# Combine weights of a top-2 expert layer: stored to DRAM from the token-major table, without a transposition on TensorE

## What is computed

```python
mod = (_silu(L0_c) @ L0_wmod).reshape(L0_c.shape[0], 6, 1, -1)
...
h = _layernorm(x, axis=-1) * (1 + ca) + sa
x = x + ga * _L0_attn_ref(h, L0_attn_w_qkv, L0_attn_w_out)     # 16 heads of 8 channels
h = _layernorm(x, axis=-1) * (1 + cb) + sb
x = x + gb * _L0_ffn_ref(h, L0_ffn_w_router, L0_ffn_w_gate, L0_ffn_w_up, L0_ffn_w_down)
...
scores = jax.nn.softmax(xf @ w_router, axis=-1)                # 8 experts
topk_w, topk_idx = jax.lax.top_k(scores, TOP_K)                # 2
topk_w = topk_w / (jnp.sum(topk_w, axis=-1, keepdims=True) + EPS)
comb = jnp.zeros((T, E), dtype=xf.dtype).at[jnp.arange(T)[:, None], topk_idx].set(topk_w)
h = jax.nn.silu(g) * u                                         # per expert, 176 hidden
out_e = jnp.einsum('eth,ehd->etd', h, w_down)
y = jnp.einsum('etd,te->td', out_e, comb)
```

## Time and profile before

| what | value |
|---|---|
| median of 3 runs | 687.15 us (686.04 to 687.64) |
| span of the profiled execution | 679.4 us |
| its own time | not listed apart; the median is 7.75 us above the span |
| TensorE busy | 618.9 us (91%) |
| VectorE busy | 550.1 us (81%) |
| ScalarE busy | 450.5 us (66%) |
| GpSimd busy | 267.2 us (39%) |
| transfers | 65.58 MB in 48972 packets, 97 GB/s |

### The profile page before, as it was taken

One profiled execution on the slowest core, in us unless ns is written; L12 is line 12 of the kernel. 1 busy time (PEld: TensorE's weight loads), 2 busy tenths in 40 slices (PEclk: granted clock), 3 DMA queues, 4 the chain that ended last, 5 costly groups with the idle time before them and its releaser, 6 DMA issues.

```text
span 679.4 us, 13009 instructions
## 1 busy us (share of the span) xinstructions
PE 618.9 (91%) x3413; PEld 285.7 (42%) x3413; DVE 550.1 (81%) x1065; ACT 450.5 (66%) x859; POOL 267.2 (39%) x384
## 2 busy tenths in 40 slices
PE   5299999999999999999999999889899999999995
PEld 3112223323323322322322322225667777777773
DVE  3698889899888988988988988714788888888885
ACT  2107878778778778778778777876554555555553
POOL 4522022222222222222122122333567776776773
PEclk9658999999999999999999999979899999999999
DMA  7703505304304304303403400253334454345411
GB/s 183 197 31 82 183 3 117 106 20 106 117 19 95 126 17 95 127 17 79 143 18 72 150 18 4 76 167 109 92 114 139 137 142 141 130 137 150 136 35 31
DMA packets 48972, 65.58 MB, mean 97 GB/s; under 512 B 9432, under 2 KB 30432, under 8 KB 48928
## 3 DMA queue, kind: packets, MB, share of 16 engines
q1 hardware_dynamic: 46304, 64.32, 33.1%
q10 hardware_dynamic: 2624, 0.79, 0.5%
HBM read 47.26 MB, written 17.83 MB: 96 GB/s over the span
## 4 chain that ended last, share of the span: by engine, by line
PE 34%; DVE 20%; issue 19%; POOL 16%; ACT 5%; DMA 2%; SPq 1%; DVEq 1%; POOLq 0%; ACTq 0%
POOL hid_lo L612 13%; DVE negmax L864 13%; PE o_acc L1172 11%; PE s_row L1149 10%; PE s_col L1162 5%; ACT probs L656 3%; DVE probs L1042 1%; POOL h_lo L618 1%; PE misc L1130 1%; PE misc L1103 1%; PE misc L1100 1%; SPq L325 1%; DVE sums_inv L883 1%; DVE k_rest L878 1%; PE misc L1126 1%
## 5 line engine op out<-in xcount | busy, mean ns | idle before, releaser
L864 DVE TENSOR_REDUCE negmax<-s_row 128x1 f32<-128x512 f32 x512 | 323.0, 683 | 47.5 <-PE s_row L1149 41.9
L656 ACT ACTIVATE probs<-s_col 128x512 f32<-128x512 f32 x512 | 270.8, 599 | 76.4 <-PE s_col L1162 73.4
L1149 PE MATMUL s_row<-k_stack,q_stack 64*128 64x512 bf16 x512 | 141.7, 402 | 25.2 <-DMA k_stack<-k_scr 11.6
L612 POOL TENSOR_TENSOR hid_lo<-probs,hid_hi 128x512 fp32r<-128x512 f32 x87 | 128.5, 1493 | 61.9 <-ACT hid_hi L800 61.9
L1162 PE MATMUL s_col<-q_stack,k_stack 64*128 64x512 bf16 x512 | 132.4, 383 | 7.1 <-ACT probs L656 6.5
L1172 PE MATMUL o_acc<-probs,v_aug 128*32 128x512 f32 x1024 | 138.1, 612 | 0.0
L800 ACT ACTIVATE hid_hi<-probs 128x512 fp32r<-128x512 f32 x88 | 55.6, 632 | 85.0 <-DVE probs L1042 84.6
L1149 PEld LDWEIGHTS s_row<-k_stack,q_stack 64*128 64x128 bf16 x512 | 34.9, 93 | 180.1 <-DVE negmax L864 142.1
L1042 DVE TENSOR_TENSOR probs<-probs,q_stack 128x512 f32<-128x512 f32 x56 | 62.5, 1116 | 15.7 <-POOL hid_lo L612 13.6
L520 POOL CAST negmax_parts<-negmax 128x16 bf16<-128x16 f32 x32 | 6.3, 196 | 163.0 <-DVE negmax L864 163.0
L1032 DVE TENSOR_TENSOR probs<-probs,s_col 128x512 f32<-128x512 f32 x88 | 59.6, 677 | 2.9 <-ACT probs L820 1.6
(11 more groups left out here) (134 smaller groups left out, 713.9 us busy)
## 6 DMA issues: line engine op xcount, KB each, us to landing
q_scr<-q_parts SPq DMA_DIRECT2D x48, 128.0 KB, 2.4
k_scr<-k_parts SPq DMA_DIRECT2D x48, 128.0 KB, 2.4
q_stack<-q_scr SPq DMA_DIRECT2D x8, 768.0 KB, 6.1
k_stack<-k_scr SPq DMA_DIRECT2D x8, 768.0 KB, 7.5
q_stack<-combT_scr SPq DMA_DIRECT2D x24, 256.0 KB, 3.4
k_stack<-combT_scr SPq DMA_DIRECT2D x16, 224.0 KB, 2.9
q_stack<-combT_scr SPq DMA_DIRECT2D x16, 192.0 KB, 2.7
q_stack<-combT_scr SPq DMA_DIRECT2D x16, 160.0 KB, 2.6
```

What stands on the lines that cost most here:

```text
L612: nc.gpsimd.tensor_tensor(hid_lo[k % HIDDEN][:], weighed[(par + k) % 2], hid_hi[k % HIDDEN][:], ALU.subtract).then_inc(s["hid_split"], 1)
L656: nc.scalar.activation(probs[t % 2][:, j, :], s_col[score_bank("col", u)][:], ACT.Exp, scale=INV_SCALE).then_inc(s["exp_done"], 1)
L864: nc.vector.tensor_reduce(negmax[n % 2][:, j, qc:qc + 1], s_row[score_bank("row", u)][:], AX.X, ALU.max, negate=True).then_inc(s["row_max" ...
L1149: nc.tensor.matmul(s_row[score_bank("row", u)][:], q_stack[par][at:at + KS, head // 2, P * qc:P * (qc + 1)], k_stack[par][at:at + KS, head ...
```

## The change

The store of the combine weights reads `comb` itself: for each of the 4 chunks one transfer whose source is [128 tokens, 8 experts] and whose destination is `combT_scr` by expert, so consecutive elements of four bytes lie 2 KB apart in DRAM. The task `combT` is taken out of both tables, with TensorE's transposes, ScalarE's copy, the tile `combT` and the semaphore `combT_ready`. SyncE waits for `comb_step` instead, GpSimd's `combine` waits for the stores of the batch before, and every wait on `combT_kept` counts four transfers a batch.

```diff
@@ TASKS, OUTPUT, TAIL_AT
-        (12, 1): "max0", (15, 0): "combT",
+        (12, 1): "max0",
-    OUTPUT = ("o0", "o1", "o2", "o3", "attnT", "proj", "x1T", "router", "combT")
+    OUTPUT = ("o0", "o1", "o2", "o3", "attnT", "proj", "x1T", "router")
-               (6, 1): "x1T", (7, 1): "router", (10, 1): "combT"}
+               (6, 1): "x1T", (7, 1): "router"}
-        combT = sb("combT", [E, N])
@@ SyncE
             def keep_combT(b):
-                sp.wait_ge(s["combT_ready"], b + 2)
+                sp.wait_ge(s["comb_step"], 2 * (b + 1))
                 sp.sem_inc(s["waited"])
-                sp.dma_start(combT_scr[bass.ds(b, 1)].rearrange("o e n -> e (o n)"), combT[:]).then_inc(s["combT_kept"], 16)
+                with nc.allow_non_contiguous_dma(reason="4096 weights, by expert in DRAM"):
+                    for k in range(CH):
+                        sp.dma_start(combT_scr[bass.ds(b, 1), :, P * k:P * (k + 1)].rearrange("o e p -> p (o e)"), comb[:, k, :]).then_inc(s["combT_kept"], 16)
...
-                        sp.wait_ge(s["combT_kept"], 16)
+                        sp.wait_ge(s["combT_kept"], 16 * CH)
...
-                        sp.wait_ge(s["combT_kept"], 16 * (b + 1))
+                        sp.wait_ge(s["combT_kept"], 16 * CH * (b + 1))
@@ GpSimd
-                pool.wait_ge(s["combT_ready"], b + 1)
+                if not (isinstance(b, int) and b == 0):
+                    pool.wait_ge(s["combT_kept"], 16 * CH * b)
@@ ScalarE
-                elif name == "combT":
-                    act.wait_ge(s["misc_full"], use + 1)
-                    if not (isinstance(b, int) and b == 0):
-                        act.wait_ge(s["combT_kept"], 16 * b)
-                    nc.scalar.activation(combT[:], misc_f[0:E, :], ACT.Copy).then_inc(s["combT_ready"], 1)
@@ TensorE
-                elif name == "combT":
-                    pe.wait_ge(s["comb_step"], 2 * (b + 1))
-                    for k in range(CH):
-                        last = nc.tensor.transpose(misc_f[0:E, P * k:P * (k + 1)], comb[:, k, :], ident[:])
...
-                        if not first:
-                            pe.wait_ge(s["combT_ready"], b)
...
-                    free(B - 1, "combT")
+                    free(B - 1, "router")
...
-                    free(B - 2, "combT")
+                    free(B - 2, "router")
```

More of the change, by code:

```diff
@@ L280, in adaln_block @@
             r_max_ready r_logit_ready r_exp_ready r_sum_ready r_inv_ready r_score_ready r_sorted_ready
-            r_top_ready r_without_ready r_den_ready r_den_inv_ready comb_step combT_ready combT_kept
+            r_top_ready r_without_ready r_den_ready r_den_inv_ready comb_step combT_kept
             h_loaded h_high h_split gate_ready up_ready gate_acted gated_ready weighed_ready
@@ L729, in block_high @@
                 nc.scalar.activation(h_hi[par][:], h_raw, ACT.Copy).then_inc(s["h_high"], 1)
-            act.sem_inc(s["combT_ready"])
             act.wait_ge(s["mod_ready"], 1)
@@ L1087, in free @@
                     pe.wait_ge(s["r_logit_ready"], b + 1)
-                elif name == "combT":
-                    pe.wait_ge(s["combT_ready"], b + 2)
             def task(b, par, name):
```

## The result

| | median of the runs | lowest to highest | profiled execution: time, span | granted clock |
|---|---|---|---|---|
| before | 687.21 us (4 runs) | 686.04 to 687.64 | -, 679.4 us | 0.966 |
| changed | 796.39 us (4 runs) | 794.49 to 802.2 | 794.49 us, 792.7 us | 0.900 |

The ratio is 1.1626, with a 95% interval of 1.1558 to 1.1695: the changed kernel is slower by 109 us (796.39 - 687.21).

A forecast was written before the change was run, and what follows sets the result against it. VectorE's row maxima, waiting on TensorE's scores, bound attention; TensorE is nearly full in the experts. Gains 0.3 + 0.3 + 0.4 = 1.0 us, addition 0: 687.15 - 1.0 = 686.2 us, range 683.2 to 695.0.

The forecast's parts named there:

- What is removed: TensorE's transposes and ScalarE's copy, in passes, last pass and first expert block: 1.0 us gained, ends 0 and 3.8.
- equal length of slots 15 and 7: Attention pass: both 2.70 us, with and without transposes, so a transposition costs VectorE nothing by slot length, 0.32 us at most.
- Rival C: Transpositions cost all of VectorE's idle time: 3.8 us gained, 683.4 us; chance 0.22.
- What is added: SyncE's four stores of 1,024 four-byte elements: 6.4 us of drain, taken as covered, cost 0.
- The price of an element: Time of one four-byte element on each transfer engine: 25 ns taken, between rows giving 21 and 51 ns.
- Where the stores lie: Stores issued at 147.25 us, gone by 154.6; 6.8, 9.8 and 10.5 us of cover before maxima and q stores.
- The tail: Last four stores lie ahead of block 2's h2T fetch on SyncE's queue: costed at nothing, 6.4 us at worst.
- Rival A: Added stores collide with ScalarE's maxima store, holding ScalarE 1.2 us past its read-back in the passes: 692.5 us; chance 0.24.
- Rival B: Elements at 80 ns delay q stores and `k_stack`, 6.5 us past slot 8 in five passes: 718 us; chance 0.10.
- The range: For 8 in 10: 683.2 to 695.0 us, taking in A with longer stalls and C, leaving out B.

The follow-up runs named there:

- rows: Changed kernel, but `comb` stored as it lies, one transfer of 128 rows of 128 bytes (weights then read in wrong order): 686.19 us, ratio 1.0005.
- add4: Kernel before, complete, plus the change's four element-wise stores of `comb` a batch to a spare DRAM tensor: 807.2 us, ratio 1.1802.
- add1: Kernel before, complete, plus one of the four element-wise stores, 1,024 elements a batch, to spare DRAM: 758.94 us, ratio 1.1066.
- to_sbuf: As add4, but the 4,096 elements a batch go to a spare SBUF tile at a pitch of 8 bytes: 683.77 us, ratio 0.998.
- pitch64: As add4, but consecutive tokens lie 64 bytes apart in spare DRAM, one element per 64-byte block: 690.29 us, ratio 1.0075.
- local: As add4, but a token's 32 weights lie together, 8 bytes apart, in spare DRAM: 777.31 us, ratio 1.1308.
- one: As add4, but a single transfer of 4,096 elements a batch, a token's 32 weights written before the next token's: 856.7 us, ratio 1.2494.

## Why the prediction was wrong, step by step

**What is removed** was right in kind, and its size can't be checked so finely. Forecast 1.0 us of gain; `rows` has it without the addition and shows 1.0005 of the time before, with 0.39% to either side, which holds 1.0 us and nothing alike. (One execution doesn't tell 0.2% from no change, as the prediction had it: the 23 of the kernel before beside `rows` run from 681.18 to 691.25 us.) The reasoning by the equal length of slots 15 and 7 was borne out: 2.70 us before, after and in `rows`. Rival C (3.8 us gained) would be 0.9945 and lies outside the interval.

**What is added** is the term that failed: "the cost of the addition is 0 in the forecast", and `add4` measures it at 121 us. It failed twice over. *The price of an element* was taken as a constant of 25 ns, with "no row excludes that, so the upper end is open beyond 51". There is no such constant: the first 2,382 packets went at 24 ns, the rest at 101, 53 on average. That the first part meets the 25 and the average the 51 is luck; neither row had stores of neighbouring single elements, and the reason for the lower, that `comb` lies on all partitions, was worth nothing. *The end of a store*, taken to be when its packets are through, is the larger error and was no term at all. In `add1` the packets were through at 281.5 us and a later store landed at 295.60; in the changed kernel the maxima landed 9 us after the drain. All the covers worked out in "Where the stores lie" were measured against the drain, and so were too long by that. (By its own numbers the drain, to 154.6, already reached past the maxima's store at 154.09.)

**Where the stores lie** had the right order of the queues and of who would be hit first, ScalarE's store at the second task. It had SyncE's q stores next at the same distance; they are issued at 164.84, because the q parts they take are made by ScalarE, which stood until 162.72. It left out the loop's turns, where ScalarE stood for 27.7 us in all, as inferred for its own next instructions. The tail, "at nothing" or 6.4 us, was 11.5 us in its longest wait for h2T.

**Rival A** (chance 0.24) named the mechanism: a wait of the exponentials for `max_scr` in the pass. It priced it at 1.2 us, from the one collision that the trace had the earlier trace rows, a store beside large loads; the four waits behind the elements are 53.9 / 4 = 13.5 us on average. **Rival B** (0.10) put the turning point at 60 ns and its damage on `k_stack`; that wait was 11.6 us once before and is 12.1 us once after, so it isn't where the time went. Rival A's size was the error, not its place.

**The range** was the last failing. The text said that the upper end of the price was open, and then closed the range at 695.0 us with 0.36 on slower. An unbounded cost on a queue that six passes depend on should have moved the forecast too. The Trainium skill's page (DMA: Bandwidth & Descriptors) was weighed there for both sides: its small packet of about 10.5 ns ("Bandwidth") is about what `add1`'s packets took, 15.6% x 16 x 3 / 1,040 = 7 ns each, and says nothing of the landing; its advice against one descriptor per element ("Rules for kernel authors") gave the right sign, though `to_sbuf` costs nothing and `pitch64` 5.7 us. Its read-modify-write below 512 B ("Specifications") doesn't decide by size alone: the rows of 128 bytes of `rows` cost nothing measurable.

## What to carry to other kernels

Before a transposition is moved into a transfer, look at what its writes do in DRAM: single elements that come to lie side by side, several in 64 bytes, held up the report of a store on another queue by 9 us (`add1`) and 15 us (the changed kernel), and as inferred the loading of instructions too, while the byte count and even the packets' time looked small. Take the cost of a store from its landing and that of the stores behind it, not from its packets; if no row of the trace has such a store, measure one before anything is built on it. And TensorE work that lies in TensorE's own wait for another engine is nearly free: removing 0.6 us of it from each pass left the slot at 2.70 us and gained nothing measurable here.

## What the runs showed of the hardware that was not expected

- 1,024 elements of four bytes, 4 KB, stored to neighbouring places of DRAM: packets through within 2.7 us, the landing of a 12 KB store behind them 16.8 us after their issue. As `add1` has 16 writes in each block, this would be about 1 us for each write after the other in one block; that is an estimate from this one run, and `local` and `one` weren't fitted to it.
- 4,096 such elements a batch in places 64 bytes apart cost 5.7 us over eight batches, and in SBUF nothing measurable. Only 4, 8, 32 and 64 bytes were tried. If it is a piece that counts, its size isn't known; the cost falls between 8 bytes (+93 us) and 32 (+10 us) of distance.
- In the changed kernel VectorE and ScalarE stood for up to 6.6 us at signals for which the profile finds no instruction ("remote"), again while such stores drained; the kernel before has no such wait. Open.
- At a loop turn ScalarE stood still for up to 13.7 us ("issue") while such stores drained. That its instructions were fetched behind them is inferred from the wait and from the time of q14's packet, not tested.
- Open: why `one` costs 50 us more than `add4`, and why the addition alone costs 12 us more than the change.
